# Prefetch hints for the branches of an image loop: a deformable convolution over 32 images

## What is computed

```python
x = x + _L0_conv_ref(_gn(x), w_qkv, w_out, b_out)      # channel attention
x = x + _L1_conv_ref(_gn(x), proj_w, proj_b, off_w, off_b, mask_w, mask_b, gamma, beta)

# in _L1_conv_ref
offset = jnp.clip(_conv(x, off_w, off_b), -max_off, max_off)      # max_off = 8
mask = 2.0 * jax.nn.sigmoid(_conv(x, mask_w, mask_b))
y = _deform_conv(x, offset, mask, proj_w, proj_b)
mean = y.mean(axis=(0, 2, 3)); var = y.var(axis=(0, 2, 3))
yn = (y - mean) * jax.lax.rsqrt(var + 1e-05) * gamma + beta
return jax.nn.gelu(yn, approximate=False)
```

## Time and profile before

| | |
|---|---|
| median of 3 runs | 4275.9 us (4269.94 to 4279.64) |
| span of the profiled execution | 4284.4 us |
| PE busy | 3630.2 us, 85% |
| DVE busy | 2649.3 us, 62% |
| ACT busy | 2110.5 us, 49% |
| POOL busy | 1410.9 us, 33% |
| mean granted clock of TensorE | 0.939 |
| instruction fetches | queue q8 426 packets, 6.98 MB; queue q14 373 packets, 3.06 MB |

### The profile page before, as it was taken

One profiled execution on the slowest core, in us unless ns is written; L12 is line 12 of the kernel. 1 busy time (PEld: TensorE's weight loads), 2 busy tenths in 40 slices (PEclk: granted clock), 3 DMA queues, 4 the chain that ended last, 5 costly groups with the idle time before them and its releaser, 6 DMA issues.

```text
span 4284.4 us, 109949 instructions
## 1 busy us (share of the span) xinstructions
PE 3630.2 (85%) x38338; PEld 3094.4 (72%) x38338; DVE 2649.3 (62%) x5834; ACT 2110.5 (49%) x4790; POOL 1410.9 (33%) x1165
## 2 busy tenths in 40 slices
PE   3999898999989899998989989898998989899700
PEld 2787777877777778777777877777787777778700
DVE  3666666666666666666666666666666666666522
ACT  1555554555455455545545554554555455445432
POOL 1333332333333233333333333333333333333311
PEclk8999999999999999999999999999999999999955
DMA  2000000000000000000000000000000000000298
GB/s 59 18 27 10 28 27 20 27 27 27 10 27 27 20 27 26 27 10 27 27 20 27 26 27 16 21 27 20 27 26 27 21 16 27 27 20 16 60 361 301
DMA packets 50975, 172.85 MB, mean 40 GB/s; under 512 B 9664, under 2 KB 10880, under 8 KB 50176
## 3 DMA queue, kind: packets, MB, share of 16 engines
q1 hardware_dynamic: 39584, 136.75, 10.6%
q0 software_dynamic: 7168, 25.17, 1.5%
q10 hardware_dynamic: 3424, 0.90, 0.1%
HBM read 87.29 MB, written 75.50 MB: 38 GB/s over the span
## 4 chain that ended last, share of the span: by engine, by line
PE 63%; DVE 13%; issue 13%; ACT 4%; DMA 4%; DVEq 1%; ACTq 1%; SPq 1%; POOL 0%; POOLq 0%
PE sps L650 10%; PE acc L667 6%; PE acc L668 6%; PE acc L669 6%; PE l L578 4%; PE zps L636 3%; DVE zl L1136 3%; PE zps L640 3%; PE zps L637 3%; PE zps L638 3%; PE zps L639 3%; DMA xn<-x_scratch 2%; DVE sl L1142 2%; DVE ych L1204 2%; PE l L510 1%
## 5 line engine op out<-in xcount | busy, mean ns | idle before, releaser
L1323 POOL TENSOR_TENSOR sT<-ay,bx 128x768 f32<-128x768 f32 x768 | 1148.1, 1505 | 1615.3 <-PE sps L650 1547.9
L1142 DVE TENSOR_TENSOR sl<-sps,sh 128x384 f16<-128x384 f32 x1536 | 847.1, 552 | 743.7 <-ACT sh L887 740.3
L887 ACT CAST sh<-sps 128x384 f16<-128x384 f32 x1536 | 741.7, 483 | 915.4 <-PE sps L650 905.9
L667 PE MATMUL acc<-zh,sh 128*128 128x192 f16 x4608 | 1155.7, 251 | 0.3 <-ACT ypm L910 0.3
L668 PE MATMUL acc<-zl,sh 128*128 128x192 f16 x4608 | 1155.5, 251 | 0.0
L669 PE MATMUL acc<-zh,sl 128*128 128x192 f16 x4608 | 1155.2, 251 | 0.0
L650 PE MATMUL sps<-eye,sT 128*128 128x128 f32 x4608 | 808.0, 285 | 322.0 <-issue 218.2
L853 ACT CAST zh<-zps 128x288 f16<-128x288 f32 x1536 | 620.1, 404 | 699.6 <-PE zps L640 672.6
L1136 DVE TENSOR_TENSOR zl<-zps,zh 128x288 f16<-128x288 f32 x1536 | 693.9, 452 | 423.0 <-ACT zh L853 415.7
L650 PEld LDWEIGHTS sps<-eye,sT 128*128 128x128 f32 x4608 | 544.5, 143 | 451.9 <-issue 229.4
L667 PEld LDWEIGHTS acc<-zh,sh 128*128 128x128 f16 x4608 | 459.0, 100 | 37.5 <-issue 35.9
(11 more groups left out here) (200 smaller groups left out, 6498.0 us busy)
## 6 DMA issues: line engine op xcount, KB each, us to landing
xin<-in_x SPq DMA_DIRECT2D x32, 512.0 KB, 5.5
xin<-in_x SPq DMA_DIRECT2D x64, 256.0 KB, 5.9
x_scratch<-x SPq DMA_DIRECT2D x32, 512.0 KB, 2.8
y_scratch<-ych SPq DMA_DIRECT2D x32, 512.0 KB, 2.7
zh<-y_scratch SPq DMA_DIRECT2D x20, 512.0 KB, 11.0
zl<-x_scratch SPq DMA_DIRECT2D x20, 512.0 KB, 12.0
out<-zh POOLq DMA_DIRECT2D x20, 512.0 KB, 8.8
x_scratch<-x SPq DMA_DIRECT2D x32, 256.0 KB, 3.5
```

Of the source, the lines that this page charges most:

```text
L667: pe.matmul(acc[:, 0:C], s_h, zh[:, j, ky, z], start=start and kx == 0, stop=False)
L887: act.copy(sh[:, u % S_RING].rearrange("p k n -> p (k n)"), sps[u % 2][:, 0:3 * P]).then_inc(s_hi, 1)
L1142: dve.tensor_tensor(one(sl), sps[u % 2][:, 0:3 * P], one(sh), ALU.subtract).then_inc(s_lo, 1)
L1323: pool.tensor_tensor(sT[:, p % ST_RING].rearrange("p k (r x) -> p k r x", r=R), a, x_, ALU.mult)\
```

## The change

Each far branch gets a prefetch hint. `where_far` no longer uses `If` and `Else`: it writes the compare and branch itself, true target the near increments, with `.branch_hint(announced)`. `announced` is a place in the instruction stream that `mark_branch_hint_location()` takes at the start of unit 32 (`ANNOUNCE_FAR`) on PE, DVE and ACT; an instruction BRANCH_PREFETCH_HINT stands there, which names the branch that is to come. DVE reads the flag in unit 24 in place of 13.

The loop is written out as `pairs_of_images` in place of `Fori` on PE, ACT, DVE and POOL; SP keeps its own. Its branch gets a hint as well, marked at the end of the loop's body. `part1` now takes a range of units, FRONT (0 to 23) or BACK (24 to 47), and is called for both in turn. It has a second place for the loop's hint (`ANNOUNCE_EDGE`, unit 8), which needs an argument `edge` that no call gives.

```diff
+        @contextmanager
+        def pairs_of_images(eng, start, end):
+            name, only = f"images_{nc.next_id()}", [eng.engine]
+            count = nc.alloc_registers(f"{name}_b", engines=only)
+            nc.regs_mov(count, start)
+            nc.br(f"{name}_loop", engines=only)
+            with nc.body(f"{name}_loop", valid_engines=only):
+                edge = []
+                yield nc.snap(count, min_val=start, max_val=end - 1), edge
+                nc.regs_alu(count, count, 2, op=ALU.add)
+                eng.br_lt(count, end, on_true=f"{name}_loop", on_false=f"{name}_end").branch_hint(edge[0])
+            nc.switch_bb(f"{name}_end")
...
-            part1(0, 0, True)
-            with eng.Fori(1, NB - 2, 2) as b:
-                part1(b, 1, True)
-                part1(b + 1, 0, True)
-            part1(NB - 1, (NB - 1) % 2, False)
+            part1(0, 0, True, FRONT)
+            part1(0, 0, True, BACK)
+            with pairs_of_images(eng, 1, NB - 1) as (b, edge):
+                part1(b, 1, True, FRONT)
+                part1(b, 1, True, BACK)
+                part1(b + 1, 0, True, FRONT)
+                part1(b + 1, 0, True, BACK)
+                edge.append(eng.mark_branch_hint_location())
+            part1(NB - 1, 1, False, FRONT)
+            part1(NB - 1, 1, False, BACK)
...
+        FRONT, BACK = range(UNITS // 2), range(UNITS // 2, UNITS)
+        ANNOUNCE_EDGE, ANNOUNCE_FAR = 8, 32
...
-        def where_far(flag, eng, b, par, more, far_pass, *counts):
-            with eng.If(flag == 1):
+        def where_far(flag, announced, eng, b, par, more, far_pass, *counts):
+            name, only = f"far_{nc.next_id()}", [eng.engine]
+            eng.br_cond(flag == 0, f"{name}_near", f"{name}_pass").branch_hint(announced)
+            with nc.body(f"{name}_pass", valid_engines=only):
                 far_pass(b, par, more)
                 eng.sem_inc(far_left, 1)
-            with eng.Else():
+                eng.br(f"{name}_end")
+            with nc.body(f"{name}_near", valid_engines=only):
                 for s, n in counts:
                     eng.sem_inc(s, n)
+                eng.br(f"{name}_end")
+            nc.switch_bb(f"{name}_end")
...
-            def part1(b, par, more):
-                if first(b):
+            def part1(b, par, more, units, edge=None):
+                if first(b) and units is FRONT:
...
-                for u in range(UNITS):
+                for u in units:
+                    if u == ANNOUNCE_EDGE and edge is not None:
+                        edge.append(pe.mark_branch_hint_location())
+                    if u == ANNOUNCE_FAR:
+                        announced = pe.mark_branch_hint_location()
...
-                    if u == 13:
+                    if u == 24:
                         flag = is_far(dve, b, par)
```

More of the change, by code:

```diff
@@ L916, in part1 @@
                         part0(u, b + 1, 1 - par)
-                where_far(flag, act, b, par, more, far_pass, (fz_hi, FAR_Z), (fs_hi, FAR_UNITS), (fy_pm, TILES))
+                if units is FRONT:
+                    return
+                where_far(flag, announced, act, b, par, more, far_pass, (fz_hi, FAR_Z), (fs_hi, FAR_UNITS), (fy_pm, TILES))
             images((part0, part1, lambda: None), act)
@@ L1223, in part1 @@
                     split_s(1, b)
-                for u in range(UNITS):
+                for u in units:
+                    if u == ANNOUNCE_EDGE and edge is not None:
+                        edge.append(dve.mark_branch_hint_location())
+                    if u == ANNOUNCE_FAR:
+                        announced = dve.mark_branch_hint_location()
                     if u + 2 < UNITS:
```

22 lines of the change are left out of this document (16 added, 6 removed).

## The result

The changed kernel takes 4110.7 us, the median of three executions of 4109.4 to 4119.8 us. The kernel before took 4273.0, the median of the four on record now (the prediction had 4275.9 from three). The ratio is 0.962, 95% interval 0.961 to 0.964: about 162 us, or 3.8%, faster. A fourth execution of the changed kernel took 7424.2 us and is left out of the median and the ratio; what happened in it stays open, and the last experiment looks at one possible cause.

The account below looks back on a forecast made before the run. PE holds most of the chain, 13% of which is issue: pauses between images, fetching code behind taken branches. 52 + 52 + 8 - 2 = 110, less a little for DVE, 108 us saved: 4276 to 4168 us, range 4115 to 4250.

Parts of the forecast that it names:

- Odd seam, 15 x 3.5: Loop body's first image to second: hinted far branch shortens PE's pause, second code fetch stays; 3.5 us each, 52 in all.
- the hints' cost of 2: Loop's hint on the path, about 0.1 us 15 times: 2 us lost, bounds 0.5 and 5; far hints cost nothing.
- The clock, taken at nothing: Low clock behind seams: 36 us more saved if it holds at odd seams, or 29 us lost; counted as nothing.
- Even seam, 14 x 3.7: Second image to next loop turn: PE's near branch falls from 3.78 to 0.08 us; 3.7 us each, 52 in all.
- First image, last image and 15th end, 8: Seams of the first and last images and the loop's 15th end: 3 + 3 + 2 = 8 us saved.
- The loop's hint, nothing: Hint for the loop's closing branch: lead about 0.1 us against a fetch of 4.29, so nothing saved.
- ACT's and DVE's hints, nothing: Far hints on ACT and DVE: counted as nothing; up to 14 us at even seams if theirs fail while PE's works.
- DVE's flag in unit 24: DVE's later flag load, 0.31 us of its sequencer while PE has queued work: nothing, at most 10 us lost.
- Rival B: Part of the hinted code arrives in time, helping one seam kind mainly: 52 to 68 us saved, 4208 to 4224; chance 0.22.
- Rival D: Hint fetches at once in unit 32, displacing code about to run on PE: slower, 4340 to 4404 us; chance 0.10.
- Rival C: The hint is dropped or held for something else before the branch, no effect: 4276 us; chance 0.10.
- Rival E: Clock holds at the odd seam or loop's hint shortens its fetch: 36 to 50 us more, 4080 to 4132; chance 0.06.

Follow-up runs that it names:

- g3: Changed kernel with 254 increments of an unused semaphore on PE ahead of its loop, moving the loop's code: 4141.5 us, 0.971 of the kernel before.
- e2: Changed kernel with 247 increments of an unused semaphore on PE ahead of its loop, moving the loop's code: 4186.4 us, 0.981 of the kernel before.
- e3: Changed kernel without the hint for the loop's branch, far hints kept: 4105.1 us, 0.963 of the kernel before.
- e4: Changed kernel with the hint for the loop's branch alone, none for the far branches: 4270.0 us, 1.001 of the kernel before.
- f3: Changed kernel with the far branch hinted on PE alone, not on ACT and DVE: 4103.5 us, 0.960 of the kernel before.
- f1: Changed kernel with 120 increments of an unused semaphore at the start of PE's program, moving its code: 4110.3 us, 0.962 of the kernel before.
- g2: Last experiment: changed kernel with the flag's threshold at -1, so every image takes the far pass: 15,072.8 us in one execution.
- f4: Changed kernel with PE's far hint at the start of unit 44 in place of 32: 4122.7 us, 0.964 of the kernel before.
- f2: Changed kernel with the loop turned to end after unit 23 of an odd image, its hint at unit 8: 4028.4 us, 0.943 of the kernel before.
- g4: Changed kernel with PE's far hint at the start of unit 47 in place of 32: 4181.3 us, 0.980 of the kernel before.

## Why the prediction was wrong, step by step

The forecast sum was 110 us in the span (108 after a little for DVE), and the span fell by 175.5.

- **Odd seam, 15 x 3.5: this is the step that failed.** It gave 7.9. The working put the end of the pause at 360.5, because "that code comes 3.4 us after the landing": the second fetch was kept. It is gone with the hint (the g3 and e2 pair prices it at 2.9 us a seam, its share of the clock included). In the terms of the sum, PE's idle time fell by 5.4 us a seam where 3.5 were put, and its busy time by 2.5 where nothing was put. The first pause went nearly as worked out (1.1 us forecast to be left, 0.61 measured). 15 x 4.4 = 66 us, the whole of what was missing; the other terms nearly cancel (even seams 6 less, first and last images 2.5 more, the hints' cost of 2 not seen).
- **The clock, taken at nothing**: it is the other half of the same error. It was rightly seen that 2.4 us are lost behind each odd seam, and that it hung on whether the clock holds; with both pauses gone it does, at all 15. The page's 51.5 us less of PE's busy time are what the clock gave in all, of them 38 at the odd seams, 15 x 2.5, close to the 36 of the upper bound.
- **Even seam, 14 x 3.7**: 3.3, close, but partly by luck: only 2.7 of it is idle time, and 0.6 is the clock, put at nothing. The reasoning held (near branch nearly gone, loop's branch unchanged), with two small errors: an announced branch costs 0.36 and not 0.08 us, and at eight of the fourteen it is later than that, up to 2.1. The other way, the stretch of low clock behind it became shorter, 6.8 us for 10.2.
- **First image, last image and 15th end, 8**: 10.5. The interval behind the first image shrank by 6.0 us and the one with the 15th end of the loop by 4.9, where 3 and 3 had been put; 2.5 and 1.7 of these are busy time, again the clock. Behind the last image nothing was gained where 2 had been put: from its branch to the end it is 1.1 us more.
- **The loop's hint, nothing**: right (e3, e4), and so was its cost, which is too small to see. **ACT's and DVE's hints, nothing**: right (f3), with the 14 us that were left open not needed. **DVE's flag in unit 24**: nothing, PE's wait for `sl` is 96.1 us before and after.
- **Rival B (part of it late)** had its mechanism in the right place, the even seam, but its price of 40 us and more was far too high: the eight late branches exceed 0.36 us by 8 us in all, and f1, where the even ones are all short, is no faster. **Rival D (the hinted packet displaces code about to run)** did not happen: no pause stands between unit 32 and the seam. Its condition was worked out from a hint that is acted on at once; the trace shows that it is held, at the odd seam for 29 us (hint at 310.1, packet at 338.9), and that the fetch then takes the place of the sequential one. The pause that D feared exists where the hint is wrong (g2). **Rival C (no effect)** is what the loop's hint alone gives (e4), not the change. **Rival E** was right about the odd seam ("the clock holds"), and its 4080 to 4132 hold the time, but not by its own sum: 36 to 50 us more than forecast is 4118 to 4132, and 4080 needs both of them. It was given a chance of 0.06, since the case that both pauses go was not worked out.

The Trainium skill, "Advanced Engine Details and Errata", section ISA Cache, has "Only 2 cache lines!" beside a larger memory for TensorE. With two lines and a fetch made at the hint, one would expect rival D; the runs do not contradict the two lines, since the fetch is not made at the hint, and none of them shows their number.

## What to carry to other kernels

- Where a page shows "issue" pauses at a loop's end or behind a conditional piece of code, look at the sequencer's own rows: on PE a branch that took 3 to 4 us and not 0.1 was waiting for code, and a hint 10 us or more ahead took that to 0.4 where the branch stood deep in its packet. On ACT and DVE the row of the branch stays short, and the wait shows behind it. A hint directly ahead of its branch did nothing; if two branches stand together, move one (here the loop's end to the middle of an image: 82 us). A hint for the side that is not taken costs a fetch, so announce the side that is.
- A pause in PE was paid twice here, once in time and once in the clock behind it (5.4 and 2.5 us at an odd seam). When a change may remove all pauses of a place, work out the case that they all go, and let its chance be that of its weakest link, not a remainder.
- When a forecast keeps a cost "because its cause is still there", name what would take the cause away. Here the second fetch had the same cause as the first, the code at the landing place, and a hint for that code could well have changed both. How it did so is still open.

## What the runs showed of the hardware that was not expected

- A hint acts about when the sequencer enters the 16 KB packet that holds the branch, or, if it stands in that packet, without being held: packets moved 0.6 to 2.7 us before a branch 64 instructions in and 10.9 to 11.7 us before one 216 instructions in, against 3.5 to 3.7 us behind a hint inside (f4). So a branch near the beginning of its packet is late even with a hint 40 us ahead (3.8 and 3.5 us at 4 and 12 instructions in, f2).
- The announced packet is fetched in place of the next sequential one: 32 packets less, 16 of them back when the hint is inside (f4), and a pause of 2.0 to 2.3 us at the end of the branch's packet when the branch is not taken (g2).
- A long branch ended 2.3 to 3.1 us after its packet began to move, announced or not. That start lay 0.9 to 1.6 us behind an unannounced branch and 3.1 to 4.3 us behind a hint (g4, odd seams).
- A landing place 11 to 13 instructions short of a packet's end costs a second pause of 1.8 us without a hint and none with one; at about 20 and 24 short it costs 1.5 to 1.7 us with a hint too (e2, f2). The distances are counted, and why they matter is open.
- Semaphore increments in a row start 0.15 us apart on PE's sequencer, the four of a seam as well as the 247 (38.9 us), though each row says 0.05.
